# The last layer of a four-layer graph network: per-head products as row tiles of 32 or 64 rows instead of block-diagonal operands

## The reference

```
m      = h @ map_w.T + map_b
n      = m / |m| per head;             cos = n n^T per head (64 x 64)
q, k   = m @ q_w.T + q_b, m @ k_w.T + k_b
p      = softmax(mask(q k^T / sqrt(32))) * keep
adj    = (cos > 0.1) * p
sem    = h @ gcn_map_w.T + gcn_map_b
out    = relu((adj sem) gcn_W.T / (sum(adj) + 1));   x = x + out
```

## Time and profile before

| | |
|---|---|
| median of three runs | 2108.97 us |
| the profiled execution's own time | 2107.84 us |
| its span in the profile | 2106.0 us |
| TensorE (PE) busy over the span | 96% |
| VectorE (DVE) busy | 71% |
| ScalarE (ACT) busy | 48% |
| GpSimd (POOL) busy | 29% |
| granted clock of TensorE, mean | 0.987 |

### The profile page before, as it was taken

The page is one execution under the profiler, slowest core; times in us unless marked ns, Lnnn a source line. Parts: engine busy times, 40 slices in busy tenths (PEclk is TensorE's granted clock), DMA queues, the critical chain, the costliest instruction groups (busy, mean ns, idle before and its releaser), DMA issues. The chain is left out here.

```text
span 2106.0 us, 52874 instructions
## 1 busy us (share of the span) xinstructions
PE 2019.6 (96%) x18448; PEld 1865.0 (89%) x18448; DVE 1486.2 (71%) x3280; ACT 1019.4 (48%) x2122; POOL 609.1 (29%) x656
## 2 busy tenths in 40 slices
PE   7999999899999799999999999999999899999998
PEld 7988888799999699999999999999998788888886
DVE  7999989577777455555555555555555599999998
ACT  6777777455555322322223223222222476776675
POOL 4545555322222011011111111111111344444443
PEclk9999999899999899999999999999999899999999
DMA  3222222433223200111111001110110122112221
GB/s 107 77 68 76 64 74 76 132 101 92 82 85 91 67 24 17 32 31 31 31 31 31 26 19 31 31 31 31 31 31 21 27 63 61 53 53 61 61 61 46
DMA packets 149370, 113.31 MB, mean 54 GB/s; under 512 B 42944, under 2 KB 148800, under 8 KB 149312
## 3 DMA queue, kind: packets, MB, share of 16 engines
q1 hardware_dynamic: 149312, 112.52, 18.3%
HBM read 78.93 MB, written 33.55 MB: 53 GB/s over the span
## 5 line engine op out<-in xcount | busy, mean ns | idle before, releaser
L274 POOL TENSOR_TENSOR ln_rstd<-ln_var_eps,minus_half 128x2 f32<-128x2 f32 x128 | 90.8, 709 | 760.4 <-DVE ln_var_eps L267 759.3
L1723 ACT ACTIVATE l_cat_hi<-banks 128x512 fp32r<-128x512 f32 x128 | 76.5, 598 | 260.2 <-PE banks L1894 260.2
L182 PE MATMUL banks<-ln_hT_hi,square_w_hi_held 128*128 128x256 f32 x512 | 153.2, 299 | 5.1 <-DVE square_w_lo_held L657 3.2
L291 ACT ACTIVATE ln_h<-ln_x,ln_shift,ln_rstd 128x256 f32<-128x256 f32 x256 | 139.1, 591 | 31.5 <-DVE ln_shift L281 26.8
L182 PE MATMUL banks<-ln_hT_hi,l_g_w_hi 128*128 128x256 f32 x512 | 148.8, 291 | 4.1 <-PEq L1992 4.1
L182 PE MATMUL banks<-l_cat_hi,l_aw_hi 128*128 128x256 f32 x512 | 144.5, 282 | 0.0
L183 PE MATMUL banks<-ln_hT_lo,square_w_hi_held 128*128 128x256 f32 x512 | 144.3, 282 | 0.0
L184 PE MATMUL banks<-ln_hT_hi,square_w_lo_held 128*128 128x256 f32 x512 | 144.0, 281 | 0.0
L184 PE MATMUL banks<-ln_hT_hi,l_g_w_lo 128*128 128x256 f32 x512 | 142.6, 278 | 0.0
L183 PE MATMUL banks<-ln_hT_lo,l_g_w_hi 128*128 128x256 f32 x512 | 142.5, 278 | 0.0
L183 PE MATMUL banks<-l_cat_lo,l_aw_hi 128*128 128x256 f32 x512 | 141.6, 277 | 0.0
(11 more groups left out here) (244 smaller groups left out, 6994.1 us busy)
## 6 DMA issues: line engine op xcount, KB each, us to landing
hidden<-y SPq DMA_DIRECT2D x96, 256.0 KB, 2.1
ln_x<-hidden SPq DMA_DIRECT2D x96, 256.0 KB, 2.7
x_res<-hidden SPq DMA_DIRECT2D x96, 256.0 KB, 2.9
ln_x<-x SPq DMA_DIRECT2D x32, 256.0 KB, 2.8
x_res<-x SPq DMA_DIRECT2D x32, 256.0 KB, 3.0
out<-y SPq DMA_DIRECT2D x32, 256.0 KB, 2.1
l_adj_u<-adj SPq DMA_DIRECT2D x96, 16.0 KB, 2.3
l_stage_attnT<-L_attnT SPq DMA_DIRECT2D x4, 256.0 KB, 3.2
```

The costliest lines, as they stand in the source:

```text
L182: nc.tensor.matmul(out, lhs(lh), rhs(rh), start=start, stop=False, skip_group_check=True)
L274: self.nc.gpsimd.tensor_tensor(self.rstd[:, g.slot], self.var_eps[:, g.slot], self.core.minus_half[:, 0:PAIRS], ALU.pow).then_inc(self.rst ...
L291: last = self.nc.scalar.activation(self.h[:, u, p, :], self.x[:, u, p, :], ACT.Relu, bias=self.shift[:, u, p:p + 1], scale=self.rstd[:, u, ...
L1723: nc.scalar.activation(cat_hi[:, h * KC:(h + 1) * KC], halves(B_HP[h]), ACT.Relu).then_inc(cat_hi_ready.sem, 1)
```

## The change

`k_bd` and `n_bd` are gone. `by_head` now multiplies 32 rows x 64 tokens by 32 rows x 64 tokens for each head, board and half of the features: 32 matmuls for the scores of both tiles, 32 for the cosines. The four heads at rows 0, 32, 64 and 96 write four banks (2 to 5), scores in the columns up to 256 and cosines behind them, so the stationary and the moving operand of the cosines are both `nT`. Attend becomes 32 matmuls of 64 rows x 64 by 33 columns, the two row halves writing banks 6 and 7. The other banks are dealt anew: Q shares bank 2 with the scores and waits for their shift, K, n transposed and h transposed share bank 0, M and SEM bank 1, and the transposes of linked go to banks 6 and 7, and wait for t.

ScalarE adds the bias of k in two instructions on 128 partitions, as it does for q; exponentials of tile 1 come before q. `keep` moves from VectorE to GpSimd, ahead of the next mask. On VectorE the statistics are finished where they are begun, m comes before the second maximum, gate_output and the norms come later, and the sums stand around linked. `var_eps` (in all four layers) and `norm_cl` are written by another VectorE instruction with the same result. The zeroing of the block-diagonal tiles is dropped. `v` holds 33 columns for each head, without zeros.

```diff
@@ variance
-        nc.vector.tensor_scalar(self.var_eps[:, u], self.mean_var[:, u, :, 1], LN_EPS, None,
-                                ALU.add).then_inc(self.var_eps_ready.sem, 1)
+        var = self.mean_var[:, u, :, 1]
+        nc.vector.scalar_tensor_tensor(out=self.var_eps[:, u], in0=var, scalar=LN_EPS, in1=var, op0=ALU.add,
+                                       op1=ALU.max).then_inc(self.var_eps_ready.sem, 1)
@@ gated_graph_layer
-        k_bd = sb("k_bd", [P, 2, KC, NB, HPC, S], F32, MOVED)
-        n_bd = sb("n_bd", [P, 2, KC, NB, HPC, S], F32, MOVED)
+        k = sb("k", [P, 2, KC, TOK], F32, MOVED)
-        v_bd = sb("v_bd", [P, 2, PAIRS, 2, HH, 2, VW], F32, MOVED)
+        v = sb("v", [P, 2, PAIRS, 2, HPC, VW], F32, MOVED)
-        B_HT, B_Q, B_M, B_K, B_SEM, B_S, B_COS, B_O = 0, 1, 2, 1, 2, 3, (5, 6), 6
+        B_HT = B_NT = B_K = 0
+        B_M = B_SEM = 1
+        B_S, B_Q, B_O = 2, 2, 6
+        W = HPC * S
@@ gpsimd
-            nc.gpsimd.memset(k_bd[:], 0.0).then_inc(preset.sem, 1)
-            nc.gpsimd.memset(v_bd[:], 0.0).then_inc(preset.sem, 1)
...
+            nc.gpsimd.memset(v[:, :, :, :, :, HD:VW], 1.0).then_inc(preset.sem, 1)
...
+                if c2.exists(groups):
+                    after(pool, mask_ready, c2, apart=core)
+                    after(pool, factor_steps, c2.back(2), apart=core)
+                    nc.gpsimd.tensor_scalar(keep[:, c2.slot], mask[:, c2.slot, :, 0], 1.0 / MASKED, 1.0, ALU.mult,
+                                            ALU.add).then_inc(keep_ready.sem, 1)
@@ scalar
-                def block_diagonal_k(hp):
-                    r0 = hp * HD
-                    for c in range(KC):
-                        last = nc.scalar.activation(
...
-                def diagonal_n(hp):
...
+                def with_bias(dst, bank, a):
+                    for c in range(KC):
+                        last = nc.scalar.activation(dst[:, b1.slot, c], ps[:, bank, c * TOK:(c + 1) * TOK], ACT.Identity,
+                                                    bias=qk_bias[:, a, c:c + 1], scale=1.0)
+                    return last
...
                 if c2.exists(groups):
                     exponentials(0)
...
+                    exponentials(1)
+                if b1.exists(groups):
                     after(act, q_in_psum, b1)
                     after(act, scores_in_psum, b1.back(2))
+                    with_bias(q, B_Q, 0).then_inc(q_ready.sem, 1)
+                    after(act, k_in_psum, b1)
+                    with_bias(k, B_K, 1).then_inc(k_ready.sem, 1)
                 if gn is not None:
                     ln.apply(act, gn)
@@ vector
-            nc.vector.memset(n_bd[:], 0.0).then_inc(n_bd_zeroed.sem, 1)
...
-                    for hp in range(HPC // 2, HPC):
-                        r0 = hp * HD
-                        last = nc.vector.tensor_copy(n_bd[r0:r0 + HD, c2.slot, :, :, hp, :],
-                                                     nT[r0:r0 + HD, c2.slot].rearrange("p c (b t) -> p c b t", b=NB))
-                    last.then_inc(n_bd_dve_ready.sem, 1)
@@ tensor
-            def by_head(i, bank, stationary, moving, start, u):
-                for bb in range(2):
-                    pb = 2 * i + bb
...
+            def by_head(first_col, stationary, moving, start, u, in_psum):
+                for p in range(PAIRS):
                     for c in range(KC):
-                        last = nc.tensor.matmul(ps[bb * S:(bb + 1) * S, bank, c * HPC * S:(c + 1) * HPC * S],
-                                                stationary[:, u, c, pb * S:(pb + 1) * S], moving[:, u, c, pb],
-                                                start=start and c == 0, stop=True, skip_group_check=True)
+                        for bb in range(2):
+                            toks = slice((2 * p + bb) * S, (2 * p + bb + 1) * S)
+                            col = first_col + (p * KC + c) * S
+                            for hp in range(HPC):
+                                r = slice(hp * HD, (hp + 1) * HD)
+                                last = nc.tensor.matmul(ps[bb * S:(bb + 1) * S, B_S + hp, col:col + S],
+                                                        stationary[r, u, c, toks], moving[r, u, c, toks],
+                                                        start=start, stop=True, skip_group_check=True)
...
+            def cosines(c2, b1):
+                after(pe, nT_ready, c2, apart=core)
+                after(pe, shifted_ready, c2, apart=core)
+                after(pe, q_ready, b1, apart=core)
+                by_head(W, nT, nT, True, c2.slot, cos_in_psum)
...
+            def attend(e):
...
+                for p in range(PAIRS):
+                    for hp in range(HPC):
+                        col = (p * HPC + hp) * VW
+                        for bb in range(2):
+                            for c in range(KC):
+                                r = slice(c * S, (c + 1) * S)
+                                last = nc.tensor.matmul(ps[bb * S:(bb + 1) * S, B_O + c, col:col + VW],
+                                                        linkedT[r, u, hp // 2, hp % 2 * PAIRS + p, bb * S:(bb + 1) * S],
+                                                        v[r, u, p, bb, hp], start=True, stop=True, skip_group_check=True)
```

More of the change, by code:

```diff
@@ L1226, in step @@
                                             ALU.mult).then_inc(n_ready.sem, 1)
-            run_steps(pool, step, groups, 1)
+            run_steps(pool, step, groups, 2)
         @block.scalar
@@ L1396, in step @@
                 if c2.exists(groups):
-                    sum_of_prob(1)
-                if c2.exists(groups):
-                    link(0)
-                    link(1)
+                    softmax_shift(1)
+                if e.exists(groups):
+                    gate_output()
+                if gn is not None:
+                    ln.shifts(dve, gn)
                 if b1.exists(groups):
@@ new lines, in scores @@
+            def scores(c2):
+                after(pe, mask_ready, c2)
+                after(pe, q_ready, c2)
+                after(pe, k_ready, c2)
+                after(pe, linked_ready, c2.back(1))
+                for hp in range(HPC):
+                    for r in (slice(0, S), slice(S, P)):
+                        nc.tensor.matmul(ps[r, B_S + hp, 0:W], core.ident_bf[:, r],
+                                         mask[:, c2.slot].unsqueeze(2).to_broadcast([P, PAIRS, KC, S]),
+                                         start=True, stop=False, skip_group_check=True)
+                by_head(0, q, k, False, c2.slot, scores_in_psum)
@@ L1478, in transpose_linked @@
+            def cosines(c2, b1):
[3 more added lines that the diff above has]
+                by_head(W, nT, nT, True, c2.slot, cos_in_psum)
             def transpose_linked(c2, i):
                 after(pe, linked_ready, c2, i + 1)
+                after(pe, t_ready, c2.back(1))
                 li = linked[:, c2.slot, i].rearrange("p h t -> p (h t)")
[L1481 to L1482 removed]
+                for j in range(2 * PAIRS):
+                    last = nc.tensor.transpose(ps[:, B_O + i, j * P:(j + 1) * P], li[:, j * P:(j + 1) * P], core.ident)
@@ L1499, in step @@
                 if c2.exists(groups):
-                    scores(c2, 0)
+                    scores(c2)
                 if e.exists(groups):
-                    u = e.slot
-                    after(pe, linkedT_ready, e)
-                    after(pe, sem_ready, e)
-                    after(pe, t_ready, e.back(1))
-                    for p in range(PAIRS):
-                        for bb in range(2):
-                            for j in range(HH):
-                                last = nc.tensor.matmul(ps[bb * S:(bb + 1) * S, B_O + p, j * 2 * VW:(j + 1) * 2 * VW],
-                                                        linkedT[:, u, p, j, bb * S:(bb + 1) * S], v_bd[:, u, p, bb, j],
-                                                        start=True, stop=True, skip_group_check=True)
-                    last.then_inc(o_in_psum.sem, 1)
-                if c2.exists(groups):
-                    scores(c2, 1)
+                    attend(e)
+                if b1.exists(groups):
+                    after(pe, ln.hT_hi_ready, b1)
+                    after(pe, ln.hT_lo_ready, b1)
+                    after(pe, sem_ready, b1.back(1))
+                    project(2, b1, B_M).then_inc(m_in_psum.sem, 1)
                 if c2.exists(groups):
```

178 lines of the change are left out of this document (63 added, 115 removed).

## The result

The kernel after the change takes **2077.35 us** (median of 4 runs, 2072.99 to 2078.38) against 2108.76 (4 runs), a ratio of 0.9845, 95% interval [0.9833, 0.9857]. Forecast were 2076 us and a range of 2062 to 2096. The profiled execution took 2077.76 us, its span is 2075.8 (before: 2107.84 and 2106.0).

What follows compares the result with a forecast made beforehand. VectorE was taken to bound the loop at 13.7 us a step, TensorE close behind. Loop -26.4, start -2 and end -4 make -32.4 us from 2107.84, so 2075.4, stated as 2076 us; range 2062 to 2096.

Steps and rivals of the forecast that it cites:

- VectorE bounds the loop: Last layer's steady loop: VectorE sets the pace at 13.7 us a step, TensorE close behind; 12.84 after the change.
- -0.96 for copies and keep: VectorE's list: the two copies into l_n_bd and keep go, saving 0.96 us a step.
- +0.15 for the dependent wait: VectorE: the aggregation now waits for the statistics right before it, costing 0.15 us a step, bounds 0 and 0.3.
- The waits for ln_x: VectorE: 1.2 us of waits in some 22 steps may be covered, taking the step's saving from 0.81 to 0.85 us.
- Operands on two banks: 0: VectorE: maximum, shift and linked spanning two banks cost 0, bounds -0.1 and +0.3 us a step.
- (a): TensorE rival: row tiles take turns, steps of 14.2 to 14.5 us, +12 to +21, 2125 us; chance 0.11.
- (b): TensorE rival: whole engine starts a record only every 0.022 to 0.028 us, 2097 us at the middle; chance 0.07.
- 9.9 us of work: TensorE per step after the change: 12.8 less 3.2 plus 0.3 us, hidden behind VectorE's 12.84.
- rival (c): Half a success: row tiles overlap, but TensorE at 77% busy loses clock (2092 us) or cosines wait (2085); chance 0.10.
- The hole ahead of the cosines, 1.5 us, slack 0.7: TensorE waits some 1.5 us for shift and q, free; cosines end 0.7 us before VectorE wants them for linked.
- ScalarE 0 in the loop: ScalarE: eight copies of k, 3.33 us, become two, 0.84; no bound in the loop, so 0.
- Start -2, end -4: Ends of the layer: earlier k gives -2 us, fewer copies and shorter cosines -4 us, bounds -2 and -5.

Runs made afterwards that it cites:

- r0: The changed kernel run again unaltered, as the measure for the other runs on the same chip; 2074.37 us, 0.9839 of the kernel before.
- e5: Changed kernel with the end of the LayerNorm statistics (aggregation and var_eps) moved behind the bias of m; 2071.37 us, 0.9823 of the kernel before.
- e10: Changed kernel with v's evacuation moved from VectorE to ScalarE, its bias added by two bf16 matmuls; 2073.38 us, 0.9827 of the kernel before.
- e9: Changed kernel with 20 matmuls that nobody reads added on TensorE ahead of the cosines; 2107.19 us, 0.9986 of the kernel before.
- e2: Changed kernel with scores and cosines both issued one row tile at a time (head outermost); 2085.21 us, 0.9888 of the kernel before.
- e4: Changed kernel with the cosines alone issued one row tile at a time (head outermost); 2077.75 us, 0.9855 of the kernel before.
- e3: Changed kernel with the scores alone issued one row tile at a time (head outermost); 2075.13 us, 0.9836 of the kernel before.
- e6: Changed kernel with 8 matmuls that nobody reads added on TensorE ahead of the cosines; 2075.38 us, 0.9841 of the kernel before.
- e8: Changed kernel with both the later LayerNorm statistics and the 8 unread matmuls ahead of the cosines; 2070.16 us, 0.9818 of the kernel before.

## Why the prediction was right, point by point

- **VectorE bounds the loop; -0.96 for copies and keep.** Right as to the list, but half of the picture: the ring through the load is as long as the list, before as after, and the term holds because copies and keep stood in the part that both share. The copies alone put back cost +27 us, and the step fell by 0.89 (0.97 in r0) where 0.85 was said; -27.5 us in the loop against -26.4.
- **+0.15 for the dependent wait.** Too low, in bounds: the next instruction used to start 0.67 us behind the statistics, and the aggregation starts 0.91 behind them (1858.14 to 1859.05), +0.24. In before:

```profile
1857.39 0.75 DVE L256 BATCH_NORM_STATS2 ln_stats<-ln_x 128x6 f32<-128x256 f32 x2
1858.06 0.16 DVE L1346 TENSOR_TENSOR l_kept<-banks,l_keep 128x16 f32<-128x16 f32 x1
```

  It was mostly balanced by norm_cl, which y used to follow 0.26 us behind its start, and which the sum now follows after 0.10.
- **The waits for ln_x, "which the new place may cover".** Wrong. They did not go (1.8 us in 19 steps after, 1.0 in 18 before), and I read them as noise where they were the mark of the ring. The term was 0.04 us a step, so the sum did not suffer; the step of 12.6 at the low end of my range was open, as e5 shows with 12.57. Had the change taken its 0.96 us between y and the statistics instead, by e10 next to nothing of the gain would have come.
- **Operands on two banks: 0.** Right, 0.68, 0.69, 1.28 us.
- **TensorE's blocks.** Row tiles overlap, rivals (a) and (b) fall: 0.011 us between records for scores and cosines, (1.14 - 0.22)/63 = 0.015 for attend. Rival (b) took the floor of about 25 ns between two starts, from the Trainium skill, "TensorE: Matmul & The Clock Gate", section "Wait — 56ns, not 53.3ns?", for the whole engine; across tiles these spacings are below it. But 9.9 us of work was mis-sized: from the starts of the blocks scores, attend and cosines take 0.99 + 1.06 + 0.84 = 2.89 us where 1.92 + 0.3 was said, and before it was 13.69 less the one hole of 0.41, 13.3, not 12.8. 13.3 - (5.08 - 2.89) = 11.1, e9 gives 11.2, and TensorE is busy for 88% of the loop (220 of 250 us), not the 77% of rival (c). TensorE therefore had 1.5 us to spare and not 3. The sum did not need them; e2 and e9 show how near the edge was.
- **The hole ahead of the cosines, 1.5 us, slack 0.7.** Measured 1.40, with q as its releaser, and linked 0.5 us behind the cosines' end.
- **ScalarE 0 in the loop.** Right for the old step, wrong for the new one: with k in pieces the step is 13.3 us. The price of an edit was read against the bound of before, not against the bound that the other edits make.
- **Clock (rival c).** Three short drops, 2.8 us, in the change's profile, one each in r0 and e4, none in e2, e3, e5, e6 and e8.
- **Start -2, end -4.** Measured -1.1 and -1.6; the first differs from run to run (the first copy starts at 1667.5 in r0, 1668.3 in e3, 1665.8 in e4), so its size is open. At the start k came earlier, but the first maximum only moved from 1664.91 to 1664.65, since v stands ahead of it and waited for SEM:

```profile
1662.90 1.73 DVE L1399 TENSOR_TENSOR l_v<-banks,l_sem_bias 64x256 f32<-64x256 f32 x4 [1.98 <-PE banks L184]
1664.65 0.69 DVE L1302 TENSOR_REDUCE l_smax<-banks 128x8 f32<-128x512 f32 x1
```

  At the end the cosines take 0.92 us in place of 3.30, but what follows is slower: the granted clock there is 0.75 against 0.89. Before, the lower level of 1.2 GHz fell on the cosines, behind the hole of 2.83 us, and it was back at 1.00 from 2098 us; now it is at 0.50 from 2066 us on, behind holes of 1.89 and 1.80 us, and falls on the two blocks that follow.

```profile
2063.35 0.92 PE L1443 MATMUL banks<-l_nT 32*64 32x64 f32 x64 [1.89 <-ACT l_nT L1270]
2066.07 1.97 PE L1472 MATMUL banks<-constants_sb,l_linked 128*128 128x128 f32 x8 [1.80 <-DVE l_linked L1316]
2068.72 1.94 PE L1486 MATMUL banks<-l_v,l_linkedT 64*64 64x33 f32 x64 [0.69 <-ACT l_linkedT L1257]
```

  In before these two blocks read:

```profile
2097.16 1.57 PE L1482 MATMUL banks<-constants_sb,l_linked 128*128 128x128 f32 x8
2099.41 1.55 PE L1509 MATMUL banks<-l_v_bd,l_linkedT 128*64 128x66 f32 x32 [0.69 <-ACT l_linkedT L1260]
```

  They take 0.4 us more each; and linked waits for its turn in VectorE's list. This term, over by 3.3 us, is the largest error of the sum; the loop's 1.1 the other way took back a third of it.
- **The sum.** It is nearer than its terms, and that part is luck. In r0, with less of the lower clock, the loop is 30.0 us shorter (423.1 to 393.1) where -26.4 was said, and start and end are 0.5 and 1.6 where 6 was said: errors of 3.6 and 3.9 us against each other.

## What to carry to other kernels

Before you price a shorter list on the bounding engine, follow each ring that goes through it, queues included: a load that stands behind a store of the step's result in one queue makes a ring of store, load and compute, and a wait of a few tenths in a few steps marks it. Then look where the work stands that you take away: beside the transfer it brought nothing here, behind it it counted in full. Price an edit against the bound that the whole change leaves, not against the present one, and take TensorE's spare time from its holes, since my sum of blocks had it twice as large as it was. Where array tiles are small, issue them in rotation over the row tiles as well as the column halves.

## What the runs showed of the hardware that I had not expected

- f32 records on tiles of 32 rows x 64 columns in rotation over eight places started 0.011 us apart on the mean, on 64 x 64 in four places (33 columns each) 0.015; ordered by row tile the same records were 0.021 apart, not the 0.030 of the earlier trace rows where only column halves alternate.
- An instruction on VectorE that reads the result of the one right before it cost 0.24 us more than an independent one (statistics to aggregation: it starts 0.91 us behind their start, where the independent one started 0.67 behind it).
- A maximum, a shift and a product whose operand spans two banks took the same time as in one bank, to 0.01 us.
- A load of 256 KB behind a store in one queue was first used 3.8 us after the end of the instruction that the store waits for: 0.24 to the store, 0.74 to the load, 2.80 to its landing (e10).
- Holes of about 1.4 us ahead of the cosines in every step left the granted clock at 0.98 to 1.00 in the loop; at the layer's end, with TensorE waiting 1.89, 1.80 and 0.69 us ahead of its last blocks, it was 0.75 over 21 us.
